# A six-layer gated recurrence on one core: how its loads, gathers, first instructions, gate transposes and last output are ordered

## The reference

```python
for i in range(n_layers):                    # 6 layers, HIDDEN = 256, VOCAB = 4000
    gate = ih[i][token]                      # one row of 256 gates per token and layer
    state = jnp.tanh(state + jnp.matmul(state, hh[i]) * gate)
```

## Time and profile before

| | |
|---|---|
| median of three runs | 63.14 us (62.12 to 63.68) |
| the profiled execution, its own time | 62.04 us |
| its span, first to last instruction | 60.2 us |
| PE, DVE, ACT, POOL busy | 52.1, 40.5, 40.0, 34.4 us |
| mean granted TensorE clock | 0.980 |

### The profile page before, as it was taken

The page is one execution under the profiler, slowest core; times in us unless marked ns, Lnnn a source line. Parts: engine busy times, 40 slices in busy tenths (PEclk is TensorE's granted clock), DMA queues, the critical chain, the costliest instruction groups (busy, mean ns, idle before and its releaser), DMA issues.

```text
span 60.2 us, 853 instructions
## 1 busy us (share of the span) xinstructions
PE 52.1 (86%) x273; PEld 43.2 (72%) x273; DVE 40.5 (67%) x60; ACT 40.0 (66%) x69; POOL 34.4 (57%) x34
## 2 busy tenths in 40 slices
PE   0879999995887999999999999999999999999000
PEld 0679888872747689896888887888878888885000
DVE  0319974429589885874977778877779777779900
ACT  0703899503329440979999888998888988852430
POOL 4076076777624990298587876667866668700000
PEclk9999999999999999999999999999999999999975
DMA  0598688898400000000000000000000000032254
GB/s 0 12 321 271 211 280 242 222 303 222 131 16 0 0 0 0 0 0 11 0 0 0 0 0 0 0 0 5 11 5 0 0 0 0 0 144 97 107 195 154
DMA packets 5380, 4.46 MB, mean 74 GB/s; under 512 B 2186, under 2 KB 4746, under 8 KB 5376
## 3 DMA queue, kind: packets, MB, share of 16 engines
q1 hardware_dynamic: 3168, 3.41, 17.7%
q0 software_dynamic: 1152, 0.73, 4.8%
q10 hardware_dynamic: 1056, 0.27, 1.9%
HBM read 8.92 MB, written 1.05 MB: 166 GB/s over the span
## 4 chain that ended last, share of the span: by engine, by line
PE 66%; DMA 12%; issue 5%; DVE 5%; ACT 4%; POOL 3%; DVEq 0%; POOLq 0%
PE prod L443 25%; PE prod L452 12%; PE turned L427 12%; PE prod L400 9%; DMA gate<-gates_dram,row_of 8%; PE turned L465 5%; DMA last_row<-gates_dram 4%; PE turned L409 4%; POOL gate L214 3%; ACT gate L256 2%; DVE prod L349 1%; DVE pre L354 1%; DVE gp L338 1%; ACT s L267 1%; ACT s L282 1%
## 5 line engine op out<-in xcount | busy, mean ns | idle before, releaser
L230 POOL TENSOR_TENSOR sl<-s,sh 128x512 fp32r<-128x512 f32 x12 | 15.5, 1291 | 6.0 <-ACT s L282 6.0
L443 PE MATMUL prod<-sh,wr 128*128 128x512 f32 x64 | 18.8, 415 | 0.0
L400 PE MATMUL prod<-w,s 128*128 128x256 f32 x64 | 15.3, 388 | 1.3 <-ACT s L267 0.6
L349 DVE TENSOR_TENSOR prod<-prod,gate_t 128x512 f32<-128x512 f32 x16 | 11.2, 700 | 6.5 <-PE prod L452 6.5
L400 PEld LDWEIGHTS prod<-w,s 128*128 128x128 f32 x64 | 12.1, 197 | 3.1 <-issue 1.7
L443 PEld LDWEIGHTS prod<-sh,wr 128*128 128x128 f32 x64 | 10.9, 189 | 1.5
L282 ACT ACTIVATE s<-pre 128x512 f32<-128x512 f32 x16 | 9.9, 620 | 2.6 <-DVE pre L354 2.6
L354 DVE TENSOR_TENSOR pre<-prod,s 128x512 f32<-128x512 f32 x16 | 11.1, 693 | 0.6
L214 POOL DMA_INDIRECT gate<-gates_dram,row_of x8 | 8.1, 1010 | 5.6 <-issue 2.0
L452 PE MATMUL prod<-sl,wr 128*128 128x512 f32 x32 | 10.0, 395 | 0.0
L427 PE MATMUL turned<-ident,gate 128*128 128x128 f32 x64 | 9.4, 272 | 0.0
(11 more groups left out here) (20 smaller groups left out, 26.6 us busy)
## 6 DMA issues: line engine op xcount, KB each, us to landing
w<-hh_dram SPq DMA_DIRECT2D x5, 256.0 KB
s<-state_t_dram SPq DMA_DIRECT2D x4, 256.0 KB, 3.3
out_t_dram<-s SPq DMA_DIRECT2D x4, 256.0 KB, 2.0
w<-hh_dram ACTq DMA_DIRECT2D x1, 256.0 KB
gate<-gates_dram,row_of POOLq DMA_INDIRECT x8, 3.2
last_row<-gates_dram ACTq DMA_DIRECT2D x1, 6.0 KB, 2.5
tok<-token_dram SPq DMA_DIRECT2D x1, 4.0 KB, 1.7
```

The lines of the kernel that those rows point to most:

```text
L230: nc.gpsimd.tensor_tensor(of_unit(sl[:, l % 2], h, c), of_unit(s, h, c), of_unit(sh[:, l % 2], h, c).bitcast(f32), ALU.subtract).then_inc( ...
L349: nc.vector.tensor_tensor(prod_bank[u][:, :], prod_bank[u][:, :], gate_t[:, u], ALU.mult).then_inc(unit_gated[u], 1)
L400: last = nc.tensor.matmul(prod[q][:, t, :], of_quarter(s, q)[:, c, t * P:(t + 1) * P], w[:, l, c, :], start=c == 0, stop=c == KC - 1)
L443: nc.tensor.matmul(prod_bank[u][:, :], wr[:, l, k, half, c * P:(c + 1) * P], of_unit(sh[:, (l - 1) % 2], h, k), start=half == 0 and k == 0 ...
```

## The change

Five things are changed.

- Loads: each load on SP after the first two waits for the one directly before it; in the kernel before two or three were under way together.
- Gathers: tiles 0 and 1 (now `EARLY_TILES`) are gathered in two pieces. The first half of a row (layers 0 to 2) is fetched first, as before without waiting for a copy; the rest (layers 3 to 5) is fetched after all other tiles, over copies that ACT makes of the last row (two more ACT instructions). The predicated copies on DVE shrink from four (two of 512 and two of 1024 elements per partition) to three of 512.
- First instructions: DVE clears a blank tile, and PE multiplies it by itself nine times with 64 columns, where it made five transposes of the identity.
- Wide stage: from layer 3 on, PE transposes the gates of all four units of a layer in one go ahead of the four products; before, a unit's transposes stood behind each product. `gate_t` is held twice, and the order on ACT follows.
- End: the last unit's tanh and its output go in two pieces of 256 columns.

The diff, cut to its core:

```diff
 # SP
-                sp.wait_ge(state_in[0], 16)
+                sp.wait_ge(state_in[1], 16)
                 load_state(2)
-                sp.wait_ge(w_in[0], 16)
+                sp.wait_ge(state_in[2], 16)
                 load_state(3)
-                sp.wait_ge(state_in[1], 16)
+                sp.wait_ge(state_in[3], 16)
                 load_weights(1)
...
+                for l in range(2, LAYERS):
+                    sp.wait_ge(w_in[l - 1], 16)
                     load_weights(l)
...
+                            sp.dma_start(out_v[h, c, :, 0:QB], of_unit(s, h, c)[:, 0:QB]).then_inc(out_done, 16)
+                            sp.wait_ge(end_s, 1)
+                            sp.dma_start(out_v[h, c, :, QB:HB], of_unit(s, h, c)[:, QB:HB]).then_inc(out_done, 16)
 # POOL
+                pool.wait_ge(halves_ready, 1)
+                for t in EARLY_TILES:
+                    gather_early(t)
                 pool.wait_ge(rows_ready, 1)
-                for t in range(TILES):
+                for t in range(len(EARLY_TILES), TILES):
                     gather(t)
+                for t in EARLY_TILES:
+                    gather_rest(t)
                 for l in range(2, LAYERS):
                     low_weights(l)
 # ACT
-ACT_FILLS = [(1, 2, 1), (2, 2, 1), (1, 3, 1), (2, 3, 1), (1, 4, 2), (2, 4, 2), (1, 6, 2), (2, 6, 2)]
+ACT_FILLS = [(1, 2, 1), (2, 2, 1), (1, 3, 1), (2, 3, 1), (1, 4, 2), (2, 4, 2), (1, 6, 2), (2, 6, 2), (2, 0, 2)]
...
+                nc.scalar.copy(gate[:, 0:len(EARLY_TILES), HALF:HALF + HIDDEN],
+                               spread[1][:, HIDDEN:2 * HIDDEN].unsqueeze(1).to_broadcast([P, len(EARLY_TILES), HIDDEN]),
+                               ).then_inc(filled_act, 1)
...
+                        nc.scalar.activation(s_u[:, 0:QB], pre_u[:, 0:QB], ACT.Tanh).then_inc(unit_s[u], 1)
+                        nc.scalar.activation(s_u[:, QB:HB], pre_u[:, QB:HB], ACT.Tanh).then_inc(end_s, 1)
 # DVE
+                nc.vector.memset(blank[:, :], 0.0).then_inc(blank_ready, 1)
...
-                patch(1, 0, 2)
+                patch_rest()
                 gating(2)
                 sum_up(1)
                 sum_up(2)
-                patch(2, 0, 2)
                 gating(3)
 # PE
-                for _ in range(WARM_UP):
-                    nc.tensor.transpose(turned[0][:, 0, 0:P], ident[:, :], ident[:, :])
+                pe.wait_ge(blank_ready, 1)
+                for _ in range(WARM_UP):
+                    nc.tensor.matmul(turned[0][:, 0, 0:P // 2], blank[:, :], blank[:, 0:P // 2], start=True, stop=True)
...
-                for l in range(WIDE, LAYERS):
+                for l in range(WIDE + 1, LAYERS):
                     for h in range(HALVES):
-                        l_next, h_next = (l, 1) if h == 0 else (l + 1, 0)
+                        for c in range(KC):
+                            turn_gates(l, h, c)
+                    for h in range(HALVES):
                         for c in range(KC):
                             wide_product(l, h, c)
-                            if l_next < LAYERS:
-                                turn_gates(l_next, h_next, c)
```

More of the change, by code:

```diff
@@ L83, in recurrent_cells @@
         row_of = sb("row_of", [P, TILES], i32)
[L85 removed]
+        half_of = sb("half_of", [P, TILES], i32)
+        is_last = sb("is_last", [P, len(EARLY_TILES)], i32)
+        blank = sb("blank", [P, P], f32)
         last_row = sb("last_row", [P, LAYERS, KC], f32)
@@ L118, in recurrent_cells @@
         rows_ready = sem("rows_ready")
+        halves_ready = sem("halves_ready")
+        early_in = [sem(f"early_in{t}") for t in EARLY_TILES]
+        blank_ready = sem("blank_ready")
         patched = sem("patched")
@@ L208, in _, with gather_early, gather_rest @@
                                         base=0, pattern=[[-1, P]], channel_multiplier=1).then_inc(ident_ready, 1)
+                def gather_early(t):
+                    nc.gpsimd.indirect_dma_start(
+                        gate[:, t, EARLY], None, half_table,
+                        bass.IndirectOffsetOnAxis(half_of[:, t:t + 1].bitcast(u32), 0),
+                        bounds_check=last_half_fetched, oob_is_err=False,
+                    ).then_inc(early_in[t], 16)
+                def gather_rest(t):
+                    pool.wait_ge(filled_act, ACT_COUNT)
+                    nc.gpsimd.indirect_dma_start(
+                        gate[:, t, REST], None, half_table,
+                        bass.IndirectOffsetOnAxis(half_of[:, t:t + 1].bitcast(u32), 0),
+                        element_offset=HALF, bounds_check=last_half_fetched, oob_is_err=False,
+                    ).then_inc(gate_in[t], 16)
                 def gather(t):
-                    if t not in LATE_TILES:
-                        pool.wait_ge(filled_dve, fills_of(t, DVE_FILLS))
-                        pool.wait_ge(filled_act, fills_of(t, ACT_FILLS))
+                    pool.wait_ge(filled_dve, fills_of(t, DVE_FILLS))
+                    pool.wait_ge(filled_act, fills_of(t, ACT_FILLS))
                     nc.gpsimd.indirect_dma_start(
@@ L316, in fill, with patch, patch_rest @@
                     nc.vector.tensor_copy(filled(i, t, count), filling(i, count)).then_inc(filled_dve, 1)
-                def patch(i, t, count):
-                    for late in range(t, t + count):
-                        dve.wait_ge(gate_in[late], 16)
-                    nc.vector.copy_predicated(filled(i, t, count),
-                                              is_last[:, t:t + count].unsqueeze(2).to_broadcast([P, count, PIECE * HIDDEN]),
-                                              filling(i, count)).then_inc(patched, 1)
+                def patch(t):
+                    dve.wait_ge(early_in[t], 16)
+                    nc.vector.copy_predicated(gate[:, t, 0:PIECE * HIDDEN], is_last[:, t:t + 1].to_broadcast([P, PIECE * HIDDEN]),
+                                              spread[0]).then_inc(patched, 1)
+                def patch_rest():
+                    dve.wait_ge(filled_act, ACT_COUNT)
+                    tiles = slice(0, len(EARLY_TILES))
+                    nc.vector.copy_predicated(gate[:, tiles, PIECE * HIDDEN:HALF],
+                                              is_last[:, :].unsqueeze(2).to_broadcast([P, len(EARLY_TILES), HIDDEN]),
+                                              spread[1][:, 0:HIDDEN].unsqueeze(1).to_broadcast([P, len(EARLY_TILES), HIDDEN]),
+                                              ).then_inc(patched, 1)
                 def gates_of(n, first, count):
@@ L417, in turn_gates @@
                     pe.wait_ge(gated[2 * h + 1], 1)
-                    if h == 0:
-                        pe.wait_ge(patched, l // PIECE + len(LATE_TILES))
+                    if h == 0 and l < LAYERS // 2:
+                        pe.wait_ge(patched, len(EARLY_TILES) + 1)
+                    elif h == 0:
+                        for t in EARLY_TILES:
+                            pe.wait_ge(gate_in[t], 16)
                     if l == WIDE:
@@ L491, in _ @@
                 turn(7)
-                for l in range(WIDE, LAYERS):
+                wide_product(WIDE, 0, 0)
+                wide_product(WIDE, 0, 1)
+                turn_gates(WIDE, 1, 0)
+                turn_gates(WIDE, 1, 1)
+                wide_product(WIDE, 1, 0)
+                wide_product(WIDE, 1, 1)
+                for l in range(WIDE + 1, LAYERS):
                     for h in range(HALVES):
-                        l_next, h_next = (l, 1) if h == 0 else (l + 1, 0)
+                        for c in range(KC):
+                            turn_gates(l, h, c)
+                    for h in range(HALVES):
                         for c in range(KC):
                             wide_product(l, h, c)
-                            if l_next < LAYERS:
-                                turn_gates(l_next, h_next, c)
 def kernel(r_state, r_token, L0_rec_ih, L0_rec_hh):
```

76 lines of the change are left out of this document (44 added, 32 removed).

## The result

The changed kernel takes 66.90 us (median of four runs, 65.77 to 68.29) against 62.84 us (four runs of the kernel before, 62.12 to 63.68). The ratio is 1.055, 95% interval 1.039 to 1.071: it is slower. The forecast was 64.5 with a range up to 67.0: the sign and the mechanism held, its size did not. The profiled execution took 65.77 us, of which 64.0 are span (before: 62.04 and 60.2). Here and in the experiments a ratio leaves out every run that lies over 1.5% above the fastest of its own kernel, so it is not the quotient of the medians; in the changed kernel these are the runs of 68.03 and 68.29, both at a mean granted clock of 0.954 where the other two had 0.994 and 0.997.

What follows compares the result with a forecast made beforehand. PE was taken to bound the wide stage, which moves as a block with its start. 62.04 + 2.05 (single loads) - 0.2 (end) = 63.9 profiled; with half of the 1.10 to the median, forecast 64.5, range 60.9 to 67.0.

Steps and rivals of the forecast that it cites:

- Loads one at a time: SP's chain of seven loads: w5 lands at 24.2, its rounding on ACT delays `tanh(3)` and `plain(7)`, wide stage 2.05 later.
- third rival: Serial loads on SP, 2.5 to 3.0 each, w5 at 23.5 to 27: 63.1 to 66.7 on the profiled scale; chance 0.43.
- My value is built from a small load and the rate ... together 2.6: One 256 KB load on SP: 1.7 for a small load plus 0.88 at 297 GB/s; seven take 18.2.
- each 0.1 on one load is 0.7 here: SP's chain of seven loads: 0.1 us more on each load makes 0.7 us in all.
- a rival of its own at 3.3 for all seven: Gathers stretch each load on SP to 3.3, w5 lands at 29.1: 68.8 profiled, median 69.3; chance 0.07.
- Rival 1: Lone loads on SP land in 2.0 to 2.15 and the gathers' gain shows: 60.2 profiled, median 60.7; chance 0.20.
- What the gathers give back: Gathers with fewer loads beside them land sooner: stage 2 1.65 earlier if loads do not hold it; taken as 0.
- Warm-up: PE's eighteen passes end at 3.0 or 4.9, costing the copies 0 or up to 1.6; taken as 0, -0.5 to +0.5.
- POOL and the copies on ACT: Later low weights on POOL covered by 0.35; two more ACT copies, 1.7 us, fit in 3.11 of idle: cost 0.
- Wide stage: Layers 3 to 5 on PE: same work, 28.76, loop margin 0.5, cost 0; ends -0.1 and +1.
- Rival 5: The granted clock falls in the wide stage's lumps of transposes: 65 or more; chance 0.03.
- End: Last tanh and output in two pieces: half-size output 0.44 less, issued 0.1 to 0.35 late; -0.2, between -0.4 and +0.3.

Runs made afterwards that it cites:

- Experiment 8: Changed kernel, loads still single, with w5 rounded on ACT behind `tanh(4)` and its low part on POOL behind `low_state(1)`; 62.93 us, ratio 1.016 to the kernel before.
- experiment 9: Kernel before with loads one at a time and w5 rounded behind `tanh(4)`, its low part behind `low_state(1)`; 64.68 us, ratio 1.032.
- experiment 10: Changed kernel, loads still single, with w5 rounded behind `tanh(4)`, four blank products instead of nine and the output whole; 64.24 us.
- experiment 12: As experiment 10, but the six full-row gathers fetch 256 bytes of each row instead of 6 KB, so its output differs; 62.63 us, ratio 1.012.
- experiment 1: Changed kernel with the loads on SP overlapping as in the kernel before, all else changed; 63.50 us, ratio 1.020 to the kernel before.
- experiment 4: Changed kernel with loads and warm-up both as in the kernel before, the rest changed; 62.24 us, ratio 0.999 to the kernel before.
- experiment 11: Changed kernel with the loads overlapping as before, four blank products instead of nine and the output whole; 61.42 us, ratio 0.989 to the kernel before.
- experiment 3: Changed kernel with the five transposes of the identity as warm-up in place of the nine blank products; 66.46 us, ratio 1.067 to the kernel before.
- experiment 5: Kernel before with the new wide stage alone (transposes in lumps of sixteen, turned gates held twice, new order on ACT); 61.45 us, ratio 0.990.
- experiment 6: Kernel before with only the end split in two pieces; 62.64 us, ratio 1.010.
- experiment 2: Kernel before with only the loads on SP changed, each waiting for the one ahead; 68.04 us against 62.91 for the kernel before.
- Experiment 7: As experiment 4, but the output whole and the two rest gathers put behind the low weights on POOL; 61.58 us, ratio 0.990 to the kernel before.

## Why the prediction was right, and where it was off

*Loads one at a time.* The mechanism was right in each link: the seven loads, the rounding of w5, `tanh(3)`, `plain(7)`, and the wide stage moving as a block. Experiment 8 shows it by moving the rounding of w5. On the scale of the profiled execution the forecast was 63.9 and 65.77 was measured, inside its third rival (63.1 to 66.7, chance 0.43). That the median of 66.90 is still inside the range, by 0.1, owes something to luck: the wide stage gave 0.5 that the sum had at 0, and so hid part of the miss. The step that was off is the term "My value is built from a small load and the rate ... together 2.6". It measured 2.88 in the changed kernel, so w5 landed at 26.21 and not 24.2, and the term is +4.0 where 2.05 stood. The prediction's own "each 0.1 on one load is 0.7 here" gives 2.0 for the 0.28: the gap is this one number. From the landing to `tanh(3)` it is 0.55 (0.60 was summed), and `plain(7)` follows 0.76 behind that (0.77 was taken).

*Why 2.6 was too low.* Seven loads took 20.1 where 18.2 was summed. More than half of that is the plain load itself: w4 took 2.59, but w5, with no gather issued beside it, 2.78, and five of the seven 2.75 on average, 0.15 above the value built from a small load and a rate. The rest is two loads that took 3.1 and 3.3. The prediction kept stretched loads for a rival of its own at 3.3 for all seven; the runs show that it falls on some of them, up to 4.0 for w1 in experiments 9 and 10. Gathers are one cause (experiment 12), but not every load beside them is stretched.

*Rival 1, loads alone are quick*, had the outputs' 2.0 for it. No load of the seven, in any kernel with single loads, was under 2.5. The direction of the page that the prediction named (the Trainium skill, "DMA: Bandwidth & Descriptors", Latency and other measured facts) agrees with the traces: 2.6 to 2.8 for a load with little beside it, and 3.3 to 4.6 with other loads beside it. Whether a lone load has less latency or merely more of the rate, no row tells. And the gain per load is far smaller than what is lost by queuing seven of them.

*What the gathers give back* was 1.65 "if the loads do not hold it". Its first link is real: tile 3's gather is issued at 10.45 in the changed kernel and in experiment 1, and the `gating(1)` that waits for it starts at 13.81 beside single loads and at 14.87 beside overlapping ones. From this gather's issue to that start it was 3.3 to 3.9 in the six kernels with single loads and full rows, and 3.4 to 6.0 in the seven with overlapping loads. But the quicker gathers come only with the single loads, and these take more than they give. With the loads overlapping, experiments 4 and 11 gain nothing beyond the wide stage (`gating(1)` at 13.43 and 14.01, 13.19 before), so the half rows alone are worth nothing that can be measured, and the full 1.65 never showed.

*Warm-up.* The eighteen passes end at 5.0: the upper of the two ends, not the lower. "Both lie under the wait for w2 to w5, so I take 0" held: experiment 3 gains nothing. With the cover gone it is 1.26 (experiment 1 against 4), within the "up to 1.6".

*POOL and the copies on ACT* were covered, as summed: the low weights of layer 5 ran at 26.93, right behind w5's rounding, and ended at 28.21; the first low state, at 28.50, had to wait for its own tanh (27.81 to 28.42) in any case.

*Wide stage.* Predicted 0, measured -0.49 in the changed kernel and -0.36 in experiment 5, whose ratio is 0.990. The margin of 0.5 held: PE was busy 28.26 of 28.27. That the products themselves would be quicker, by some 0.03 a unit, could not be read from the rows of before. Rival 5 is refuted: 1.00 throughout, so the rule on transposes that the prediction named (the Trainium skill, "TensorE: Matmul & The Clock Gate", Part 4: PE-mode transpose) did not bite here, with sixteen of them in 1.75 us.

*End.* Predicted -0.2, measured +0.2 (+0.15 in experiment 6), inside its bounds. The error is in halving the output: 128 KB landed in 1.9 (median of the two pieces, from the page) where 256 KB took 2.0, not 0.44 less, and the second piece is issued 0.37 behind the first.

*The sum* with measured terms: 62.04 + 4.1 - 0.5 + 0.2 = 65.8, and the profiled execution took 65.77. The prediction had no term for idle PE's clock, which cost 1.7 in the profiled execution of experiment 2; in that of the changed kernel it cost nothing.

*Left open.* Why `sum_up(2)` begins up to 2.4 us after the recorded end of its turn in four kernels. Experiment 7 moved the rest gathers and it was on time, but so it was in experiments 8, 10, 11 and 12, which did not move them. And why the loads of one kernel differ from those of the next by up to 1.2 us at the same place.

## What to carry to other kernels

A load that is taken off its neighbours gets faster (2.6 to 3.3 us here, against 3.3 to 4.6), but a queue of seven pays its full duration seven times; so count the chain's landings against the first use of each, and allow for some of them being stretched by what runs beside. Then ask which of the waits ends last: of the four roundings that waited in the changed kernel, only the last one held the run. Look, too, at what stands in an in-order queue behind the instruction that waits for the load: here a conversion that nobody needed yet stood ahead of a tanh that everybody needed. And where one part of a change is covered only by another part's delay (the warm-up by the loads), mend and time them together.

## What the runs showed of the hardware

- A 256 KB load with nothing large beside it took 2.6 to 2.8 from issue to landing; beside gathers of 6 KB rows from 2.82 to 3.99, and 2.68 in the same place when the gathers' rows were 256 bytes.
- Half the bytes hardly shorten a store: 1.9 for 128 KB, 2.0 for 256 KB.
- Gathers tend to be stretched by loads as well: from the issue of tile 3's gather to the start of its consumer it was 3.3 to 3.9 beside single loads (six kernels) and 3.4 to 6.0 beside overlapping ones (seven).
- PE idle for 2.45 us (experiment 2) and for 2.17 us (experiment 3) was followed by 3.4 us at a granted clock of 0.50; sixteen transposes in 1.75 us left it at 1.00. In the changed kernel 2.21 of idle did not lower it in the profiled execution, so the length of the gap alone does not decide.
- Passes of 64 columns in float32 came 0.22 apart (4.10 over 18), hardly quicker than the transposes of 128 columns behind them (2.77 over 12, 0.23): half the columns did not halve the time.
- The six 512-column matmuls of a unit took 1.36 to 1.38 with the transposes in lumps of sixteen and 1.39 with four ahead of each unit; why, no run here tells.
